# Eleven nodes instead of twelve in the window of a half row's counts, in a two-network graph kernel

## What is computed

```python
# L0: relational graph convolution, D_FF = 286, two relations
norm_x = ln_weight * (x * rsqrt(mean(x**2) + 1e-6))
out = norm_x @ W_root + bias
for r in range(2):
    w = (edge_type == r)
    sums = segment_sum(norm_x[src] @ W_rel[r] * w[:, None], dst)
    cnt = segment_sum(w, dst)
    out = out + sums / maximum(cnt, 1)[:, None]
x = layernorm(x + (x + elu(out) @ wo_weight))
# L1: three layers over the same edges, width 256
h = relu(layernorm(x) @ W1 + b1) @ W2 + b2
for i in range(3):
    z = h + segment_sum(h[src], dst)
    h = h + relu(layernorm(relu(z @ Wa[i] + ba[i]) @ Wb[i] + bb[i]))
delta = relu(h @ Wd1 + bd1) @ Wd2 + bd2
out = layernorm(x + layernorm(x + delta))
```

## Time and profile before

| what | value |
|---|---|
| median of three runs | 612.47 us (612.41 to 612.57) |
| profiled execution, its own time | 612.71 us |
| its span in the trace | 610.7 us |
| PE (TensorE) busy | 571.9 us, 94% of the span |
| DVE busy | 395.1 us, 65% |
| ACT busy | 225.0 us, 37% |
| POOL busy | 107.7 us, 18% |
| DMA moved | 30.73 MB, 50 GB/s |

### The profile page before, as it was taken

One profiled execution on the slowest core, in us unless ns is written; L12 is line 12 of the kernel. 1 busy time (PEld: TensorE's weight loads), 2 busy tenths in 40 slices (PEclk: granted clock), 3 DMA queues, 4 the chain that ended last, 5 costly groups with the idle time before them and its releaser, 6 DMA issues.

```text
span 610.7 us, 8372 instructions
## 1 busy us (share of the span) xinstructions
PE 571.9 (94%) x2581; PEld 396.8 (65%) x2581; DVE 395.1 (65%) x1008; ACT 225.0 (37%) x457; POOL 107.7 (18%) x109
## 2 busy tenths in 40 slices
PE   0399999999999999999999999999999999999992
PEld 0255555555557768686688988886887877555541
DVE  6668888888885788888842023005857748665454
ACT  9133333333321454645332212103222224175555
POOL 9600000000000000000234453300211240041330
PEclk9999999999999999999999999999999999999998
DMA  9111111111003112121930000240010100021223
GB/s 275 54 35 35 35 34 34 34 34 33 26 9 84 40 35 68 35 65 45 253 123 0 0 0 1 60 156 0 2 35 0 33 2 2 1 63 38 68 68 101
DMA packets 21728, 30.73 MB, mean 50 GB/s; under 512 B 6281, under 2 KB 15987, under 8 KB 21696
## 3 DMA queue, kind: packets, MB, share of 16 engines
q1 hardware_dynamic: 21542, 30.07, 16.6%
q10 hardware_dynamic: 154, 0.26, 0.1%
HBM read 25.20 MB, written 5.12 MB: 50 GB/s over the span
## 4 chain that ended last, share of the span: by engine, by line
PE 91%; DVE 5%; POOL 1%; DMA 1%; ACT 1%; issue 1%; DVEq 0%; POOLq 0%
PE banks L686 19%; PE banks L828 11%; PE banks L914 11%; PE banks L747 11%; PE banks L659 6%; PE banks L717 5%; PE banks L850 4%; PE banks L840 4%; PE banks L776 4%; PE banks L778 4%; PE banks L757 3%; PE banks L904 3%; PE banks L721 2%; PE banks L667 1%; PE banks L732 1%; DMA cb_b<-in_L_gnn_conv_bias 1%
## 5 line engine op out<-in xcount | busy, mean ns | idle before, releaser
L686 PE MATMUL banks<-w_all,xnT 128*125 128x429 f32 x320 | 129.9, 527 | 0.0
L686 PEld LDWEIGHTS banks<-w_all,xnT 128*125 128x125 f32 x320 | 54.0, 189 | 28.9 <-issue 28.3
L747 PE MATMUL banks<-hT,w_s 128*128 128x250 f32 x320 | 68.7, 375 | 0.4 <-DVE hT L1222 0.3
L747 PEld LDWEIGHTS banks<-hT,w_s 128*128 128x128 f32 x320 | 60.3, 189 | 9.1 <-issue 2.2
L659 PEld LDWEIGHTS banks<-oh_code,oh_low 125*128 125x128 bf16 x320 | 31.2, 98 | 45.5 <-issue 43.6
L776 PE MATMUL banks<-y_hi,adj 125*125 125x288 f32 x200 | 55.2, 304 | 0.6 <-DVE small L1138 0.6
L659 PE MATMUL banks<-oh_code,oh_low 125*128 125x240 bf16 x320 | 47.7, 270 | 8.3 <-issue 8.3
L346 POOL TENSOR_SCALAR xh<-x_first,small 125x1024 f32<-125x1024 f32 x6 | 7.4, 1242 | 264.1 <-DVE adj L1166 263.9
L778 PE MATMUL banks<-y_lo,adj 125*125 125x286 f32 x200 | 53.5, 294 | 0.0
L1042 DVE TENSOR_TENSOR oh_code<-iota_c,edge 125x960 bf16<-125x960 f16 x82 | 53.4, 652 | 0.0
L1094 DVE TENSOR_TENSOR adj<-adj,banks 125x240 f32 x80 | 32.3, 404 | 25.7 <-PE banks L659 20.7
(11 more groups left out here) (191 smaller groups left out, 932.7 us busy)
## 6 DMA issues: line engine op xcount, KB each, us to landing
xt<-in_x SPq DMA_DIRECT2D x20, 448.0 KB
out_x<-ot SPq DMA_DIRECT2D x9, 448.0 KB
w_s<-in_L_gnn_W SPq DMA_DIRECT2D x5, 512.0 KB, 6.2
w_all<-in_L_gnn_W_rel SPq DMA_DIRECT2D x2, 1144.0 KB, 10.6
wd_s<-in_L_gnn_Wd SPq DMA_DIRECT2D x1, 2048.0 KB, 13.0
w_all<-in_L_gnn_W_root SPq DMA_DIRECT2D x1, 1144.0 KB, 7.4
xt<-in_x SPq DMA_DIRECT2D x20, 52.0 KB
wo_s<-in_L_gnn_wo_weight SPq DMA_DIRECT2D x1, 1024.0 KB, 6.3
```

Of the source, the lines that this page charges most:

```text
L686: ins = pe.matmul(pb[0:P, 2 + 2 * v + n, 0:FH], xnT[:, u], w_all[:, u, n * FH:(n + 1) * FH], start=(u == 0), stop=(u == KD - 1))
L747: ins = pe.matmul(pb[:, 4 + f % 2, 0:2 * P], w1_s[:, k, f * 128:(f + 1) * 128], hT[:, k], start=(k == 0), stop=(k == KD - 1))
```

## The change

One constant: a half row's window spans eleven target nodes where it spanned twelve.

```diff
--- before.py
+++ after.py
@@ -39,7 +39,7 @@
 LOW = 128
 G = E // (P * J)
 GP = G + 4
-W = 12
+W = 11
 NW = -(-N // W)
 C = T * W
 ND = N + 24
```

## The result

The changed kernel takes 610.03 us (median of six runs, 609.45 to 610.56), the kernel before 612.52 (six runs, 611.77 to 613.16): 2.5 us less, a ratio of 0.996 with a 95% interval of 0.9947 to 0.9972, that is 1.7 to 3.2 us. The forecast was 3.2 us less. These intervals hold 2.7 us as well as 3.2, so the times alone can't say whether a part of the forecast gain is missing. The two profiled executions differ by 2.8 us in their spans, and since their trace can be followed step by step, the account is made there.

The account below looks back on a forecast made before the run. TensorE was taken to bound stage 1. Shorter count products (2.82 + 0.03 us), ramp (0.22) and one-hots and additions at start and end (0.08 each) summed to 3.23 us less: 609.3 us from 612.47, range 608.7 to 610.7.

Parts of the forecast that it names:

- The bound: Stage 1: TensorE, busy 15.90 of 15.90 us in a tile, sets the time; DVE, busy 13.01, does not.
- 320 x 8.8 ns: Stage 1's 320 count products: 20 columns fewer save 8.8 ns each, 2.82 us in all.
- theory A: Formed after the profile: the float32 load starting with a row's last count product needs about 107 ns, now uncovered.
- the partial floor: Rival 1, part: the count product's own load keeps its pace at about 100 to 103 ns; 609.7 to 610.7, chance 0.09.
- the 188 ns at the lower clock: First four count products, 188 ns each at 1.2 GHz: allow a load of up to 94 ns at the upper clock.
- Start and end of the stage: Stage 1: ramp saves 0.22 us and two high one-hots 0.08 at the start; additions and one-hots 0.08 at the end.
- The sum: Whole kernel: 2.82 + 0.03 + 0.22 + 0.08 + 0.08 = 3.23 us less; by the terms' bounds 609.2 to 609.7.
- The high one-hot: Rival 2, DVE in stage 1: time per element rises from 0.52 to 1.04 ns, DVE binds, about 616.5 us; chance 0.03.
- the general path: Rival 3, relation products: other data brings line 686's form, 0.48 us instead of 0.13 each, over 750 us; chance 0.01.
- nothing was lost behind the stage: Against rival 4, part of the gain lost behind stage 1: tenths expected, a loss over 1 us has chance 0.02.
- my two cases: Start of stage 1: the clock's rise moves with TensorE's first product (taken), or stays put and costs 0.15 us.

Follow-up runs that it names:

- e1_pe220: Kernel before with count products and additions of 220 columns, but ramp and high one-hots kept at 480 and 960 elements: 610.52 us, ratio 0.9966.
- e2_pe240: Kernel before with only the additions shortened to 220; ramp, high one-hots and count products of 240 columns kept: 612.97 us, ratio 1.0005.
- e8_warm11: Changed kernel with 54 transposes of the unit matrix, written out, in TensorE's wait ahead of the first count product: 614.44 us, ratio 1.0026.

## Why the prediction was right, and where it was off

- **The bound.** TensorE sets the time in stage 1 and DVE does not: right, shown by `e1_pe220` and `e2_pe240`, in which the steps have the changed kernel's length with the short count products and before's length without them.
- **320 x 8.8 ns.** The price per product was right, 8.6 ns at the full clock. The failed step is "a shorter count product should come out of the end time in full": in the 61 steps without transposes 7.9 of the 34.4 ns are given back in the float32 instructions, 5.8 of them in the first, so that of the last product's 9 ns about 1 is left. By theory A that is the float32 load behind it, which needs 104 ns. The term was 2.85 us with its part at the lower clock and measured 2.28, 0.6 too much. I had looked for a load that binds at the count product's own pace; the one found is the next operand's, in front of the float32 products. That the count product's own load doesn't bind was right, but one reading behind it was not: the 188 ns at the lower clock are a mean with a short first distance in it. In ns the four are 158, 200, 200 and 200, so the bound on the load was 100 ns at the upper clock and not 94, and the partial floor reached to a pace of 106 and not 103. What rules it out are the distances with ten nodes, 90 ns at the upper clock and 167 at the lower.
- **Start and end of the stage.** 0.30 forecast and 0.38 in the trace; the ramp gives 0.22 and the two one-hots 0.08, and the rest lies within what executions differ by. The end: 0.08 forecast, 0.08 in this pair of traces (last float32 instruction to first relation product, 1.10 to 1.02 us). That they agree so well is luck: in the second profile of the changed kernel it is 1.40 us.
- **The sum.** 0.38 + 2.28 + 0.08 = 2.7 of the forecast 3.2 us in the trace, 2.8 in the span. The medians' 2.5 lies on it within their interval, 1.7 to 3.2 us. The time lies outside the 609.2 to 609.7 of the terms; the range holds it because it took in a load as a partial floor, and the loss that came has about that size by another way.
- **The rivals.** The load as a partial floor, with a chance of 0.09 and a time of 609.7 to 610.7, came nearest, and the measured 610.03 lies in it; its mechanism, a floor under all four products at 100 to 103 ns, was not what happened. The high one-hot kept its rate (608 ns), the general path did not run, and nothing was lost behind the stage.
- **The clock.** Neither of my two cases: the rise keeps no fixed distance from TensorE's first product, and the execution decides by more than the change moves. In the two executions compared it came 4.25 and 4.21 us behind that product, so the term came out as assumed by luck; in the second profile of the changed kernel it came 2.82 us behind.

## What to carry to other kernels

When an instruction is shortened, ask what its neighbours hide under it: a matmul also covers the load of the next operand, and only for as long as it runs itself. Here that cost 8 ns in front of the float32 products of line 686 and nothing in front of the transposes, so the place has to be measured. Compare the distance from start to start position by position in a repeated step; a loss of 6 ns in 1850 is plain there, where medians of runs that spread over 1 us don't show it. And compare two profiles of one program before small parts of the difference between two kernels are explained.

## What was not expected of the hardware

- From the start of the last count product to full pace of the float32 product behind it there are 103.5 to 104.4 ns at the 2.4 GHz level; by theory A that is the load of its operand of 125 columns, though the load's record lasts longer, 189 ns in the mean before as after. The transposes' float32 loads of 128 columns delay nothing behind a product of 93 ns, and bfloat16 ones of 128 columns bind nothing down to a pace of 90 ns.
- One-pass products of 240, 220 and 200 columns start 107.0, 98.4 and 90.3 ns apart (the third of the four), 0.41 to 0.43 ns per column. At the 1.2 GHz level they start 200, 183 and 167 ns apart (from the second of the four on), the columns divided by 1.2 GHz with nothing added.
- The rise to the 2.4 GHz level came, by the last long distance between two starts, from 2.8 us (the changed kernel run again) to 6.0 us (`e2_pe240`) behind the first count product, in kernels that start it within 0.3 us of each other, and the first two steps take 1.6 us more in the second. In this stretch the column of the granted clock shows 1.00 from the start, since the trace has no record of the clock ahead of the rise; the distance of the matmuls shows the lower level.
- Transposes alone bring the rise: in `e8_warm11` TensorE does nothing else from 17.31 us on, and at 25.41 us the distance of those of 128 columns falls from 213 to 109 ns.
